# Routing's scatters paced to two under way, and no reads of keys within the projection

## The chip, the core and the metric

One NeuronCore of a Trainium2 chip. The metric is the time of one execution on the device in microseconds (us); times of a kernel are medians of several runs. TensorE does the matmuls, VectorE and ScalarE the elementwise work, GpSimd the rest and the indirect DMAs, SyncE (SP) issues most other DMAs.

## The reference

Two transformer layers over 4096 tokens of width 256, float32. What matters here is the first: adaptive layer norm, attention with 16 heads of 16 and a linear position bias, a residual, then a mixture of 64 experts (8 chosen per token, at most 256 tokens each) beside a shared expert.

```python
h = _layernorm(x) * (1 + ca) + sa
score = q @ k.T / sqrt(D) + bias          # 16 heads, 4096 x 4096
x = x + ga * (softmax(score) @ v)
h = _layernorm(x) * (1 + cb) + sb
topk_idx, topk_w = route(h)               # sigmoid, groups, 8 of 64 experts
xe = zeros(E, CAP, H).at[sorted_e, pos].set(tok_sorted)   # each token's row to 8 places
x = x + gb * (experts(xe) weighted + shared(h))
```

The second layer (rotary attention, gated linear attention) follows in other stages that the change doesn't touch.

## The kernel before

The program is a row of stages with a barrier of all engines between them: modulation, `project_heads`, `bias_attention`, `shared_expert`, `experts`, and those of the second layer. Each stage is a block with one hand-written queue of instructions per engine; waits on semaphores set the order.

**The projection** (`project_heads`) runs over 8 chunks of 512 tokens. TensorE computes queries and keys of a chunk in four parts (0 and 1 queries, 2 and 3 keys), ScalarE copies part b to `parts[b]` once its stores of the chunk before have landed (`parts_stored[b]`), VectorE writes the low half, and SP stores both halves to `q_laid` or `k_laid` in DRAM: eight DMAs of 256 KB a chunk, in the order of parts 2, 0, 1, 3 (`store`). Behind them SP waits for part 2's stores and reads the chunk's keys of the first head group back into `keys[0]` (`fetch`): four DMAs, 54 rows by two heads by 512 keys for each half. In the first chunk the first group's queries are read as well. ScalarE stores the values.

**The attention** (`bias_attention`) runs over 8 chunks of 512 queries (c) by 4 groups of 4 heads (g), 32 steps. Step s needs the row maxima of its scores: TensorE computes score tiles into two buffers (`ps_max`, L1023) and VectorE reduces each (L971), 64 tiles a step, 16 tiles ahead of the step before. Then VectorE turns the maxima, SP writes them to `m_rows` in DRAM and reads them back into the query rows (`set_rows`, L735 and L741), and only then TensorE can score (L1039), ScalarE take exps (L836) and TensorE multiply with the values (L1054). The maxima of the next step and the exps of this one are interleaved instruction by instruction on TensorE. SP loads keys for step s+2 and values for s+1 in quarters as they come free. Each DMA queue works in order. At the start SP loads the queries of group 1, the first values, the keys of group 1, the other values, then calls `set_rows(0, 0)`.

**Routing** of chunk c-1 runs beside chunk c's attention, from c = 1 to 7, mostly on GpSimd (`route`). Its last part is `send_rows` (L610): 4 x 8 indirect DMAs, each of which sends 128 rows (one per token, 320 floats) to their places in `x_rows`. They are issued one after another; then GpSimd waits for all. Chunk 7's routing is done in `shared_expert` with the same `send_rows`.

Of the kernel before, what the change touches and what calls it, by code (L numbers as in the profile page):

```python
# [7 lines left out]
P = 128  # L8
T = 4096
# [3 lines left out]
CH = 512  # L13
NC = T // CH
# [20 lines left out]
TOPK = 8  # L35
# [117 lines left out]
H0 = 16  # L153
# [61 lines left out]
def load_key_rows(sp, keys, k_laid, g, n, done):  # L215

    for h in range(2):
        src = k_laid[g * HG + h:(g + 1) * HG:2, :, n].rearrange("a r n -> r a n")
        at = h * HALF
        sp.dma_start(keys[at:at + LAID, :, n].bitcast(F32), src).then_inc(done, 16)  # L220
        sp.dma_start(keys[at + LAID:at + KROWS, :, n].bitcast(F32), src[AUX:AUX + HD0]).then_inc(done, 16)


def load_query_rows(sp, quer, q_laid, g, n, done):

    for h in range(2):
        src = q_laid[g * HG + h:(g + 1) * HG:2, :, n].rearrange("a r n -> r a n")
        at = h * HALF
        sp.dma_start(quer[at:at + AUX + HD0, :, :].bitcast(F32), src[0:AUX + HD0]).then_inc(done, 16)
        sp.dma_start(quer[at + AUX + HD0:at + KROWS, :, :].bitcast(F32), src[AUX:LAID]).then_inc(done, 16)  # L230


def project_heads(nc, xres, mod, ident, x_in, w_in, q_laid, k_laid, v_aug, k_aux, q_aux, keys, quer):

    with ExitStack() as ctx:
# [12 lines left out]
        w_loaded, aux_set, k_fetched, q_fetched = sem("w_loaded"), sem("aux_set"), sem("k_fetched"), sem("q_fetched")  # L248
# [9 lines left out]
        assert HG <= H0 // 2  # L258
        with nc.Block() as block:
            @block.sync  # L260
            def _(sp):
# [10 lines left out]
                def store(c):  # L272
                    for b in (2, 0, 1, 3):
# [23 lines left out]
                sp.wait_ge(q_fetched, 64)  # L297
                sp.wait_ge(k_fetched, 64 * NC)
# [382 lines left out]
def bias_attention(nc, q_laid, k_laid, m_rows, v_aug, x_rows, y_rows, hT_rows, xres, mod, ident, r, slots, w_router, e_bias,  # L681
                   first_keys, first_quer):


    with ExitStack() as ctx:
# [3 lines left out]
        keys = [first_keys, sb("keys1", [P, NPR, T], F32R)]  # L689
        quer = [first_quer] + [sb(f"quer{g}", [P, NPR, CH], F32R) for g in range(1, NG)]  # L690
# [20 lines left out]
         pos_set, slots_set, scattered) = (  # L711
            sem(n) for n in ("dve_step pool_step x_added stats_set pay_set h_stored r_exped scored opened mask_set "
                             "weighted wsum_set pos_set slots_set scattered").split())
# [4 lines left out]
        with nc.Block() as block:  # L718
            @block.sync
            def _(sp):  # L720
                def load_keys(g, b):
                    load_key_rows(sp, keys[g % 2], k_laid, g, slice(b * QUART * P, (b + 1) * QUART * P),
                                  k_loaded[g % 2][b])
# [2038 lines left out]
```

## Time and profile before

| | |
|---|---|
| median of 3 runs | 5701.97 us (5696.46 to 5717.44) |
| the profiled execution's own time, its span | 5714.75 us, 5713.2 us |
| TensorE busy | 4888.2 us (86%) |
| VectorE busy | 4150.3 us (73%) |
| ScalarE busy | 3063.1 us (54%) |
| GpSimd busy | 1115.6 us (20%) |
| mean DMA rate | 74 GB/s |

The projection begins at some 33 us and ends with the barrier before 247.7 us; the attention ends at about 3372 us. A busy share is a mean over all stages; the stages have different limits, so the rows further down are read by stretch. L-numbers are lines of the kernel. "Idle before" is what an engine waited just ahead of an instruction, with what ended the wait as the profile infers it; "remote" is an end that it can't tie to an instruction.

### The profile page before, as it was taken

The page shows a single profiled execution, that of the slowest core. Times are in us where ns is not written, and L with a number is a line of the kernel's source. Part 1 is how long each engine was busy: PE and PEld are TensorE (multiplying, and loading weights), DVE is VectorE, ACT ScalarE, POOL GpSimd, SP SyncE. Part 2 cuts the span into 40 slices and gives each one's busy share as a digit, 9 for nine tenths or more (in the row PEclk, how much of TensorE's full clock was granted, in tenths as well). Part 3 has the DMA queues.
Part 4 walks back from the last instruction along what each step waited for, and adds up shares of the span by engine and source line. Part 5 has one row for each costly group of instructions (what it writes and reads, how often), then busy time and mean ns, then how long its engine had stood idle before and what let it go on. Part 6 is the DMA issues. An engine that isn't in the chain of part 4 may idle for free. (4 is left out here: it accounts for less than half of the span.)

```text
span 5713.2 us, 110761 instructions
## 1 busy us (share of the span) xinstructions
PE 4888.2 (86%) x39176; PEld 2470.0 (43%) x39176; DVE 4150.3 (73%) x5059; ACT 3063.1 (54%) x5260; POOL 1115.6 (20%) x1152
## 2 busy tenths in 40 slices
PE   5489997997988979979989787845889987999998
PEld 3233332332333323323323234633556664666666
DVE  4398996996987979969979622336766554778877
ACT  1147876886777768858767661211222223555554
POOL 0000012102110121021111201034422001444443
PEclk8678998998998989989989898977999997999999
DMA  5424322222222212212222113752211012010100
GB/s 178 128 94 129 127 71 83 77 78 63 74 69 67 70 58 76 74 56 75 73 56 73 38 33 94 237 171 76 70 53 45 1 50 83 28 28 28 28 28 20
DMA packets 238050, 422.57 MB, mean 74 GB/s; under 512 B 36889, under 2 KB 141354, under 8 KB 237440
## 3 DMA queue, kind: packets, MB, share of 16 engines
q1 hardware_dynamic: 190688, 341.85, 19.8%
q0 software_dynamic: 30048, 66.76, 3.9%
q10 hardware_dynamic: 16896, 8.39, 0.6%
q8 instruction: 262, 4.29, 0.3%
q14 instruction: 156, 1.28, 0.1%
HBM read 324.51 MB, written 129.17 MB: 79 GB/s over the span
## 5 line engine op out<-in xcount | busy, mean ns | idle before, releaser
L971 DVE TENSOR_REDUCE attn_mpart<-attn_ps_max 128x2 f32<-128x1024 f32 x2048 | 2477.2, 1224 | 434.7 <-remote 213.8
L836 ACT ACTIVATE attn_probs<-attn_ps_exp 128x512 f32<-128x512 f32 x4096 | 2231.6, 595 | 770.7 <-PE attn_ps_exp L1039 342.0
L1039 PE MATMUL attn_ps_exp<-attn_quer,attn_keys 54*128 54x512 f32 x4096 | 1571.9, 461 | 204.3 <-issue 126.4
L1023 PE MATMUL attn_ps_max<-attn_keys,attn_quer 54*128 54x512 f32 x4096 | 1535.9, 475 | 127.6 <-DVE attn_mpart L971 71.3
L1054 PE MATMUL attn_ps_out<-attn_probs,attn_vals 128*32 128x256 f32 x16384 | 1356.1, 404 | 35.0 <-ACT attn_probs L836 16.3
L1039 PEld LDWEIGHTS attn_ps_exp<-attn_quer,attn_keys 54*128 54x128 f32 x4096 | 642.6, 191 | 1095.3 <-ACT attn_probs L836 872.3
L1023 PEld LDWEIGHTS attn_ps_max<-attn_keys,attn_quer 54*128 54x128 f32 x4096 | 619.2, 195 | 202.7 <-DVE attn_mpart L971 138.4
L1054 PEld LDWEIGHTS attn_ps_out<-attn_probs,attn_vals 128*32 128x32 f32 x16384 | 327.8, 109 | 799.2 <-issue 488.3
L1586 POOL DMA_INDIRECT ra_rows<-y_rows,slots x256 | 254.6, 994 | 360.9 <-DVE ra_total L1753 289.5
L1657 PE MATMUL ra_psO<-ra_vals,ra_probT 128*128 128x256 f32 x1152 | 280.7, 390 | 27.3 <-DVE ra_probT L1831 24.4
L1717 ACT ACTIVATE ra_row<-ra_psS 128x512 f32<-128x512 f32 x112 | 66.8, 597 | 388.9 <-PE ra_psS L1638 379.5
L610 POOL DMA_INDIRECT x_rows<-route_pay,route_now x256 | 251.9, 984 | 82.9 <-issue 75.5
L1638 PE MATMUL ra_psS<-ra_kT,ra_qT 128*128 128x512 f32 x576 | 258.9, 604 | 8.2 <-DVE ra_kT L1803 6.6
L2238 POOL TENSOR_TENSOR gla_ke<-gla_kg,emask 128x512 f32<-128x512 f32 x128 | 152.2, 1217 | 521.2 <-DVE gla_kg L2464 521.2
L1657 PEld LDWEIGHTS ra_psO<-ra_vals,ra_probT 128*128 128x128 f32 x1152 | 217.7, 196 | 75.1 <-DVE ra_probT L1831 30.1
L2529 PE MATMUL gla_psP<-gla_wqkv,gla_hc 128*128 128x512 f32 x384 | 194.2, 644 | 2.5 <-ACT gla_egn L2318 2.0
L800 POOL TENSOR_TENSOR route_tok<-route_tok,mod 128x1024 f32<-128x1024 f32 x7 | 16.7, 2381 | 900.0 <-DVE route_tok L480 900.0
L2224 POOL TENSOR_TENSOR gla_qeT<-gla_ftT,gla_emr 128x512 f32<-128x512 f32 x128 | 173.0, 1384 | 14.0 <-ACT gla_ftT L2270 14.0
L1831 DVE COPY ra_probT<-ra_psT 128x512 f32<-128x512 f32 x144 | 96.8, 689 | 108.4 <-PE ra_psT L1648 87.1
L1638 PEld LDWEIGHTS ra_psS<-ra_kT,ra_qT 128*128 128x128 f32 x576 | 109.3, 195 | 135.2 <-issue 124.2
L2323 ACT ACTIVATE gla_sq<-gla_psO 128x512 f32<-128x512 f32 x32 | 19.1, 597 | 266.4 <-PE gla_psO L2637 266.4
L1725 ACT ACTIVATE ra_row<-ra_row,ra_top 128x512 f32<-128x512 f32 (+7 forms) x32 | 70.9, 2216 | 160.7 <-DVE ra_top L1823 128.7
(367 smaller groups left out, 5413.9 us busy)
## 6 DMA issues: line engine op xcount, KB each, us to landing
attn_keys<-k_laid SPq DMA_DIRECT2D x248, 304.0 KB
attn_vals<-v_aug SPq DMA_DIRECT2D x128, 512.0 KB, 15.4
attn_keys<-k_laid SPq DMA_DIRECT2D x248, 128.0 KB
x_rows<-attn_zeros POOLq DMA_DIRECT2D x16, 1280.0 KB, 11.0
exp_x<-x_rows SPq DMA_DIRECT2D x64, 320.0 KB
exp_w1w<-in_w SPq DMA_DIRECT2D x64, 256.0 KB
y_rows<-exp_y SPq DMA_DIRECT2D x64, 256.0 KB
k_laid<-proj_parts SPq DMA_DIRECT2D x32, 256.0 KB
```

What stands on the lines that cost most here:

```text
L610: pool.indirect_dma_start(out=x_rows, out_offset=bass.IndirectOffsetOnAxis(ap=r.now[:, n, k:k + 1].bitcast(U32), axis=0), in_=r.pay[:, n, ...
L836: act.activation(probs[k % 2][:, j, :], ps_exp[bank_of(g, n)][:, :], ACT.Exp).then_inc(exp_done, 1)
L971: dve.tensor_reduce(mpart[i][:, kb, TC * pair + tile::TC * NPR], ps_max[buffer][:, :, :], AX, ALU.max).then_inc(unit_read, 1)
L1023: mm = pe.matmul(ps_max[buffer][:, h, :], quer[at % NG][half(h), pair, tile * P:(tile + 1) * P], keys[at % 2][half(h), pair, kb * CH:(kb + ...
L1039: pe.matmul(ps_exp[bank_of(g, n)][:, :], keys[g % 2][half(h), pair, k * P:(k + 1) * P], quer[g][half(h), pair, :], start=True, stop=True). ...
L1054: mm = pe.matmul(ps_out[j * VW:(j + 1) * VW, n], vals[:, k, j * VW:(j + 1) * VW], probs[k % 2][:, j, n], start=(k == 0 and q == 0), stop=( ...
L1586: pool.indirect_dma_start(out=rows[n % 2][:, k, :], out_offset=None, in_=y_rows, in_offset=bass.IndirectOffsetOnAxis(ap=slots[:, n, k:k + ...
L1638: mm = pe.matmul(psS[g % 2][:, :], qT[s // TC % 2][:, k, s % TC * P:(s % TC + 1) * P], kT[:, k, b * BLK:(b + 1) * BLK], start=(k == 0), st ...
L1657: mm = pe.matmul(psO[s % 2][:, :], probT[(before(s) + b) % 2][:, j * P:(j + 1) * P], vals[:, n, :], start=(n == 0), stop=(n == TC * blocks ...
L2224: last = pool.tensor_tensor(qeT[:, b, :, :], ftT[:, 3, b, :].unsqueeze(1).to_broadcast([P, NE, P]), emr[i][:, :, :], ALU.mult)
L2238: last = pool.tensor_tensor(ke[i][:, e, :], kg2[:, :], emask[:, bass.ds(m, 1), e].to_broadcast([P, KDV]), ALU.mult)
L2529: mm = pe.matmul(ps, hc[i][:, k, :], wqkv[:, x, k, :], start=(k == 0), stop=(k == KD - 1))
```

## The change

In the attention, `send_rows` gets a function `pace`: ahead of scatter i, from the third on, GpSimd waits until scatter i-2 has landed. For this the scatters count on two semaphores in turn. The shared expert's `send_rows` uses two semaphores too, without pacing. In the projection SP no longer reads keys and queries; it stores the parts in the order 0, 1, 2, 3. The attention's start loads the first group's queries and all its keys ahead of what it loaded before; `keys[0]` and `quer[0]` are allocated there. TensorE waits for them as for all others.

```diff
             def _(sp):
...
-                def store(c):
-                    for b in (2, 0, 1, 3):
+                with sp.Fori(0, NC) as c:
+                    for b in range(NB):
                         laid = q_laid if b < 2 else k_laid
                         hold(sp, qk_parts, NB * (c + 1) + b + 1, sp_passed)
                         for i in range(NPART):
...
-                def fetch(c):
-
-                    hold(sp, parts_stored[2], 16 * NPART * (c + 1), sp_passed)
-                    load_key_rows(sp, keys, k_laid, 0, bass.ds(c * CH, CH), k_fetched)
-
-                store(0)
-                sp.wait_ge(aux_set, 32)
-                for b in range(2):
-                    sp.wait_ge(parts_stored[b], 16 * NPART)
-                load_query_rows(sp, quer, q_laid, 0, slice(0, CH), q_fetched)
-                fetch(0)
-                with sp.Fori(1, NC) as c:
-                    store(c)
-                    fetch(c)
...
-def send_rows(pool, r, x_rows, scattered):
+def send_rows(pool, r, x_rows, scattered, pace=None):
 
     for n in range(TC):
         for k in range(TOPK):
+            if pace is not None:
+                pace(n * TOPK + k)
             pool.indirect_dma_start(out=x_rows, out_offset=bass.IndirectOffsetOnAxis(
                 ap=r.now[:, n, k:k + 1].bitcast(U32), axis=0), in_=r.pay[:, n, :], in_offset=None,
-                bounds_check=SLOTS - 1, oob_is_err=False).then_inc(scattered, 16)
+                bounds_check=SLOTS - 1, oob_is_err=False).then_inc(scattered[(n * TOPK + k) % 2], 16)
...
+                load_queries(0, 0)
+                for b in range(4):
+                    load_keys(0, b)
                 load_queries(0, 1)
                 load_vals(0, 0)
                 for b in range(4):
...
-                    send_rows(pool, r, x_rows, scattered)
-                    hold(pool, scattered, SENT * c, pool_passed)
+                    def two_under_way(i):
+                        if i >= 2:
+                            hold(pool, scattered[i % 2], SENT // 2 * (c - 1) + 16 * (i // 2), pool_passed)
+                    send_rows(pool, r, x_rows, scattered, two_under_way)
+                    for i in range(2):
+                        hold(pool, scattered[i], SENT // 2 * c, pool_passed)
```

## Rows read from the trace of the kernel before

**Rows 1.** The page: costliest group (busy us, mean ns | idle before)
```profile
L971 DVE TENSOR_REDUCE attn_mpart<-attn_ps_max 128x2 f32<-128x1024 f32 x2048 | 2477.2, 1224 | 434.7 <-remote 213.8
```
**Rows 2.** Windows: stretch, length; busy us by engine; clock, DMA share, GB/s
```profile
861.00:921.00 60.00, 59.33 (x569) 21.93 (x566) 59.02 (x59) 52.08 (x97) 6.14 (x13) 1.00 0.26 78
...
921.00:981.00 60.00, 29.28 (x171) 9.85 (x171) 17.61 (x19) 15.08 (x28) 31.56 (x32) 0.57 0.25 89
...
921.00:925.00 4.00, 4.00 (x37) 1.40 (x37) 3.19 (x3) 1.83 (x4) 3.12 (x3) 1.00 0.34 124
...
925.00:931.00 6.00, 3.06 (x24) 1.02 (x22) 1.88 (x2) 2.28 (x4) 4.71 (x5) 0.73 0.45 170
...
1690.00:1750.00 60.00, 29.10 (x196) 10.28 (x195) 21.04 (x22) 17.82 (x32) 31.52 (x32) 0.66 0.13 39
...
3245.00:3255.00 10.00, 2.94 (x12) 1.06 (x12) 1.23 (x1) 0.84 (x2) 7.76 (x8) 0.50 0.03 4
```
**Rows 3.** Timeline of GpSimd: start us, us; [idle before <- what ended it]
```profile
921.04 1.13 POOL L610 DMA_INDIRECT x_rows<-route_pay,route_now  x1 [1.00 <-POOL slots L820]
...
961.07 0.98 POOL L610 DMA_INDIRECT x_rows<-route_pay,route_now  x1 [0.30 <-issue]
...
1103.90 2.37 POOL L800 TENSOR_TENSOR route_tok<-route_tok,mod 128x1024 f32<-128x1024 f32 x1 [141.85 <-DVE route_tok L480]
...
3225.49 1.10 POOL L610 DMA_INDIRECT x_rows<-route_pay,route_now  x1 [0.93 <-POOL slots L820]
```
**Rows 4.** Timeline of VectorE after the first and the last burst
```profile
966.36 1.23 DVE L971 TENSOR_REDUCE attn_mpart<-attn_ps_max 128x2 f32<-128x1024 f32 x1 [5.92 <-remote]
...
3269.91 2.36 DVE L971 TENSOR_REDUCE attn_mpart<-attn_ps_max 128x2 f32<-128x1024 f32 x2 [21.18 <-remote]
```
**Rows 5.** Timeline of the rope stage, a burst of eight gathers
```profile
4285.14 1.01 POOL L1586 DMA_INDIRECT ra_rows<-y_rows,slots  x1 [26.47 <-DVE ra_total L1753]
...
4296.42 0.69 DVE L1831 COPY ra_probT<-ra_psT 128x512 f32<-128x512 f32 x1 [5.52 <-PE ra_psT L1648]
```
**Rows 6.** DMA: software queue in 961 to 963.3, all in 963.3 to 976
```profile
q0 software_dynamic: 96, 0.00, 3.0%
...
DMA packets 1, 0.02 MB, mean 1 GB/s; under 512 B 0, under 2 KB 0, under 8 KB 0
```
**Rows 7.** Timeline of the projection: SP's issues and one ScalarE copy
```profile
102.31 1.48 SPq L279 DMA_DIRECT2D k_laid<-proj_parts  x2
...
124.68 0.64 SPq L279 DMA_DIRECT2D k_laid<-proj_parts  x1
...
122.51 1.08 ACT L322 ACTIVATE proj_parts<-proj_psQ 128x512 fp32r<-128x512 f32 x2 [5.40 <-DMA q_laid<-proj_parts]
...
213.59 1.66 SPq L279 DMA_DIRECT2D k_laid<-proj_parts  x2
...
247.72 0.32 SPq L229 DMA_DIRECT2D attn_quer<-q_laid  x1
```
**Rows 8.** Timeline of the attention's start, and a later store of m_rows
```profile
257.71 1.22 PE L1023 MATMUL attn_ps_max<-attn_keys,attn_quer 54*128 54x512 f32 x4 [48.89 <-DMA route_e_bias_wide<-in_e_bias]
...
333.23 0.58 SPq L735 DMA_DIRECT2D m_rows<-attn_mturned  x1
...
335.29 0.62 SPq L741 DMA_DIRECT2D attn_quer<-m_rows  x2
...
349.18 1.28 ACT L836 ACT_TABLE_LOAD   x1 [131.79 <-PE attn_ps_exp L1039]
...
857.01 0.55 SPq L735 DMA_DIRECT2D m_rows<-attn_mturned  x1
...
869.76 0.60 SPq L741 DMA_DIRECT2D attn_quer<-m_rows  x2
```
**Rows 9.** Windows of a chunk of the projection and of the attention's start
```profile
102.30:124.70 22.40, 13.29 (x40) 7.39 (x40) 8.54 (x20) 4.44 (x9) 0.00 (x0) 0.92 0.57 163
...
316.00:333.00 17.00, 12.01 (x32) 4.42 (x30) 16.90 (x19) 0.00 (x0) 0.00 (x0) 0.50 0.00 0
```

More of the change, by code:

```diff
@@ L212, in chunk_pairs, with project_heads @@
     return go
[L215 to L233, printed above, removed]
+def project_heads(nc, xres, mod, ident, x_in, w_in, q_laid, k_laid, v_aug, k_aux, q_aux):
     with ExitStack() as ctx:
@@ L678, with bias_attention @@
 SENT = 16 * TC * TOPK
-def bias_attention(nc, q_laid, k_laid, m_rows, v_aug, x_rows, y_rows, hT_rows, xres, mod, ident, r, slots, w_router, e_bias,
-                   first_keys, first_quer):
+def bias_attention(nc, q_laid, k_laid, m_rows, v_aug, x_rows, y_rows, hT_rows, xres, mod, ident, r, slots, w_router, e_bias):
     with ExitStack() as ctx:
@@ L688, in bias_attention @@
         sem = ctx.enter_context(fresh_semaphores(nc, "attn_"))
-        keys = [first_keys, sb("keys1", [P, NPR, T], F32R)]
-        quer = [first_quer] + [sb(f"quer{g}", [P, NPR, CH], F32R) for g in range(1, NG)]
+        keys = [sb(f"keys{i}", [P, NPR, T], F32R) for i in range(2)]
+        quer = [sb(f"quer{g}", [P, NPR, CH], F32R) for g in range(NG)]
         vals = sb("vals", [P, NT, HG * VW])
@@ L721, in load_keys @@
                 def load_keys(g, b):
-                    load_key_rows(sp, keys[g % 2], k_laid, g, slice(b * QUART * P, (b + 1) * QUART * P),
-                                  k_loaded[g % 2][b])
-                def load_queries(c, g):
-                    load_query_rows(sp, quer[g], q_laid, g, bass.ds(c * CH, CH), q_loaded[g])
+                    i, n = g % 2, slice(b * QUART * P, (b + 1) * QUART * P)
+                    for h in range(2):
+                        src = k_laid[g * HG + h:(g + 1) * HG:2, :, n].rearrange("a r n -> r a n")
+                        at = h * HALF
+                        sp.dma_start(keys[i][at:at + LAID, :, n].bitcast(F32), src).then_inc(k_loaded[i][b], 16)
+                        sp.dma_start(keys[i][at + LAID:at + KROWS, :, n].bitcast(F32),
+                                     src[AUX:AUX + HD0]).then_inc(k_loaded[i][b], 16)
+                def load_queries(c, g):
+                    n = bass.ds(c * CH, CH)
+                    for h in range(2):
+                        src = q_laid[g * HG + h:(g + 1) * HG:2, :, n].rearrange("a r n -> r a n")
+                        at = h * HALF
+                        sp.dma_start(quer[g][at:at + AUX + HD0, :, :].bitcast(F32),
+                                     src[0:AUX + HD0]).then_inc(q_loaded[g], 16)
+                        sp.dma_start(quer[g][at + AUX + HD0:at + KROWS, :, :].bitcast(F32),
+                                     src[AUX:LAID]).then_inc(q_loaded[g], 16)
                 def load_vals(g, b):
@@ L1014, in unit_half @@
                     tile, pair = divmod(row, NPR)
-                    first = isinstance(c, int) and c == 0 and at == 0
-                    if u == 0 and not first:
-                        pe.wait_ge(q_loaded[at % NG], LQ * (c + at // NG + (1 if at % NG else 0)))
-                    if row == 0 and kb % 2 == 0 and not first:
-                        pe.wait_ge(k_loaded[at % 2][kb // 2], LK * (2 * (c + at // NG) + at % NG // 2 + at % 2))
+                    if u == 0:
+                        pe.wait_ge(q_loaded[at % NG], LQ * (c + at // NG + 1))
+                    if row == 0 and kb % 2 == 0:
+                        pe.wait_ge(k_loaded[at % 2][kb // 2], LK * (2 * (c + at // NG) + at % NG // 2 + 1))
                     place = unit_place(c, g, d, u)
@@ L1196, in _ @@
                 send_rows(pool, r, x_rows, scattered)
-                pool.wait_ge(scattered, SENT)
+                for i in range(2):
+                    pool.wait_ge(scattered[i], SENT // 2)
             @block.scalar
```

22 lines of the change are left out of this document (10 added, 12 removed).

## The prediction, made before the changed kernel was run

> **What bounds the kernel now.** I read the page first: the costliest group is VectorE's maxima over the score tiles [rows 1], 2048 at 1.22 us, 2477 us of a span of 5713. The windows then say how close to that the attention runs. In a calm minute (861 to 921 us) VectorE is busy 59.0 of 60 us, so a tile per 1.23 us is the pace, and what keeps a tile from VectorE takes 1.23 us from the kernel. The minute after it (921 to 981) has VectorE busy for 17.6 us only: 3.2 of the first 4, 1.9 of the next 6, and the granted clock averages 0.57 [rows 2]. That minute loses 60 - 17.6/0.984 = 42 us of the stream. The timeline tells what else happens in it: GpSimd sends routing's 32 scatters, the first at 921.04, then one every 0.98 + 0.30 = 1.28 us, the last at 961.07 [rows 3]. There are seven such bursts in the attention (224 of the program's 256 scatters; the last 32 stand in the shared expert); the third loses 60 - 21.0/0.984 = 39 us [rows 2], the others lie between. About 7 x 41 = 287 us stand in them, 5% of the kernel.
>
> **What the stall is.** It isn't transfer: in the last attention burst DMA is busy 3% of a stretch in which VectorE works 1.23 of 10 us [rows 2]. It isn't unfinished work either: the long waits end as "remote", and at a moment that goes by the scatters. After the first burst that is 966.36, after the last (first scatter 3225.49) it is 3269.91 [rows 3, 4]. Counted from the first scatter these are 45.3 and 44.4 us, 32 x 1.40. The rope stage's gathers come eight at a time: the first at 4285.14, and a VectorE copy that waited 5.52 us starts at 4296.42, 11.3 us on, which is 8 x 1.41 [rows 5]. I read it so: one indirect DMA occupies for about 1.4 us something that the engines' releases need too; they are issued every 1.28 us, so a backlog forms from the second on, and little gets past it until it is worked off. Three scatters still let 3.2/4 = 80% of the stream by, the next five 31% [rows 2], which fits a backlog and not a fixed toll. The mechanism is inferred; its end points are rows.
>
> **The change, part 1: pacing.** Removed: nothing. Added: before scatter i (i from 2) a wait of GpSimd until scatter i-2 has landed. Behind it on GpSimd's queue stand only the later scatters and the next chunk's routing. That starts at 1103.90, the last scatter at 961.07 [rows 3]: 142 us of room, so the burst may take up to 183 us, 5.7 us a scatter, and delay nobody.
> How far apart will they be? The software queue's packets of the scatter issued at 961.07 end before 963.3; after it only one instruction packet is seen until 976 [rows 6]. So landing takes at most 2.2 us from the start. From a release to the next scatter's start GpSimd needs 1.00 us (the idle time in front of 921.04 [rows 3]). Two under way then means two per 3.2 us, 1.6 us apart, above 1.41: the backlog drains. Key traffic now goes on beside them, so landing will take longer; I allow 3.4 us, 2.2 us apart (estimate). In the middle, 1.8, a burst takes 58 us instead of 41. What share of the stream lives in it? The bounds are the 31% and the 80% above [rows 2]; I take 55%, the middle, since two of 1.4 us fill most of each 3.6 us. Lost per burst 58 x 0.45 = 26 us against 41: seven times 15 is **-105 us**. The ends: 80% over 50 us loses 10 (-217 in all), 31% over 58 loses 40 (-7). The 32 scatters of the shared expert aren't paced; their second semaphore costs nothing, since nobody waits before the end.
> The Trainium skill ("DMA: Bandwidth & Descriptors", Anatomy of one DMA) gives a DMA issued from GpSimd 2.0 us plus its bytes over 436 GB/s; for 128 rows of 1280 B that is an estimate of 2.4 us. The trace's bound of 2.2 us is near it, and by 2.4 the distance would be 1.7 us, the sum the same.
>
> **Part 2, the projection without reads.** A chunk now takes 22.4 us (SP's first store at 102.31, then 124.68) [rows 7]; in each, SP issues four key reads behind the eight stores. What these cost in the queue shows in the attention: a store of 16 KB (m_rows) is back after 2.1 us on an empty queue (333.23 to 335.29) and after 12.8 behind one quarter of keys (857.01 to 869.76) [rows 8]. A chunk is half a quarter, 6.4 us on the DMA engines that carry it; every store behind it in order is late by that, and ScalarE's copies wait for the stores (5.40 us at 122.51 [rows 7]). So 22.4 - 6.4 = 16 us without them. The lower bound by transfer: DMA is busy 57% of a chunk [rows 9], 12.8 us, of which the reads are an eighth (0.43 of 3.5 MB): 11. I take 17, between 15.5 and 20. The first store of a chunk now needs part 0 and not part 2, about 5 us earlier, once. From the last chunk's first store (213.59) to the attention's first DMA (247.72) it is 34.1 us [rows 7]; less the last two chunks' reads, 21. Sum over six intervals: 6 x 5.4 + 5 + 13 = 50 us (27 to 60).
>
> **Part 2, the attention's start.** The first score matmul now runs 10.0 us after the barrier (257.71, against SP's 247.72; released by GpSimd's small loads), m_rows goes out 85.5 us after it, and ScalarE turns to exp (its table load) at 349.18, +101.5, when sixteen tiles of the next group are done [rows 8]. SP's loads keep DMA busy until 316 (nothing from 316 to 333 [rows 9]): 68 us for four quarters of keys, queries and values. After the change the first group's queries and first quarter must come first, 12.8 us plus queries and latency: first matmul at about +21. Worse: four more quarters, 51 to 56 us, stand ahead of m_rows. TensorE and VectorE have only the sixteen tiles as cover, gone at +111 (+21 and the 91 us from 257.71 to 349.18). SP can hand m_rows over by +107, but in order it lands after the loads, at 68 + 51 to 56 + 4 for queries, about +126. Exp starts at about +131 instead of +101.5: **+30 us** (+11 if m_rows slips past, +35 at most). SP's keys for the third group are asked for after exp has begun, so the delay is paid once.
> Net of part 2: 30 - 50 = **-20 us**, between -45 and +10.
>
> **Sum.** -105 - 20 = -125. The profiled execution took 5714.75 us, span 5713.2; the median of the three timed runs is 5702, 12.8 lower. Against the median: **5577 us**.
>
> **Rivals.**
> *Pacing stops the stall altogether* (17%). For it: once nothing is queued, releases might never be late. Against: even three scatters cost a fifth. 7 x -36 and -20 give 5432; with something lost, up to 5490.
> *Pacing changes nothing* (15%). Landing in at most 2.2 us [rows 6] is less than 2 x 1.28: two under way is nearly true already, the wait may be free and the cadence stay. Then only part 2 counts: 5682, 5660 to 5712. Against it stands the 1.00 us of restart [rows 3], if GpSimd can't look ahead past a wait. The Trainium skill ("SBUF — State Buffer", SBUF: two separate sides) says that a compute operation and a DMA can't slow each other at SBUF; by it no number of scatters under way would matter. The stretch at 3% DMA [rows 2] agrees that it isn't SBUF, but there the engines do stand still.
> *The paced bursts are longer and stall as before* (18%; the other side). Place: the seven bursts. If each scatter holds the releases until the next is issued, the backlog is not the cause, and a burst of 32 x 1.6 + 4 = 55 us stands as the 45 do now: 7 x 9.5 = +67, less 20: 5749. It decides where the stream in a 58 us burst stays below 29% of its pace (42 us lost). For it: with the stream dead no keys load, so landing stays quick and the scatters close.
> *Part 2 costs* (5%): if ScalarE's or SP's own order keeps a chunk at 21 us, the projection gives 8 + 5 + 6 = 19 and the start takes 30: +11, and 5608 with the pacing, 5713 without.
>
> **How the numbers follow.** The forecast (partial relief) has 45%, its own range 5465 to 5690. About 0.5% (28 us) is what a measurement of this kernel can tell from none. Faster by more: nearly all of the 45, 17, and a little of the rest, 62%. Within: most of "changes nothing" and the edges, 18%. Slower: the 18 and some of part 2's, 20%. For 8 in 10 the range leaves out the lower half of the full relief and the top of the slower case: 5440 to 5745.
>
> **What would show it.** In the changed profile: scatters 1.6 to 2.2 us apart in the seven bursts and 1.28 in the shared expert; VectorE near 55% in a burst and few remote waits over 5 us; SP's first stores of chunks 16 to 20 us apart; the first group's m_rows over 15 us on its way, TensorE idle before the first exp. A cadence of 1.28 us with the same stall, or the same stall at 1.6, would prove part 1 wrong; chunks still at 22 us, part 2.

## The result and the profile after

The changed kernel took 5460.41 us (median of 4 runs, 5440.40 to 5491.74) against 5705.52 us (median of 4, 5696.46 to 5717.44): a ratio of 0.9559, 95% interval 0.9522 to 0.9596. That is 245 us less, where the prediction had 125 us less as the likeliest and 5440 to 5745 as its range. The profiled execution took 5440.40 us, span 5438.8; its span is 274.4 us below that of the profiled execution before.

The page's costliest groups after the change (line, engine and operation | busy us, mean ns | idle us before it and what ended it):

```profile
L956 DVE TENSOR_REDUCE attn_mpart<-attn_ps_max 128x2 f32<-128x1024 f32 x2048 | 2468.3, 1224 | 205.9 <-PE attn_ps_max L1007 188.3
...
L577 POOL DMA_INDIRECT x_rows<-route_pay,route_now x256 | 252.4, 986 | 455.5 <-DMA x_rows<-route_pay,route_now 375.9
```

VectorE's maxima are the same work (1224 ns each, as in [rows 1]), but the idle time in front of them falls from 434.7 to 205.9 us: 229 us less in that one row, and the 213.8 us of "remote" are no longer named. GpSimd now waits 376 us for the landings of its own scatters. Windows of the changed kernel, for a calm minute, the first two bursts, the last one in the attention and the stretch behind it (length; busy us of TensorE's matmuls, its weight loads, VectorE, ScalarE and GpSimd; granted clock, DMA share, GB/s):

```profile
841.00:901.00 60.00, 59.50 (x567) 21.93 (x567) 58.98 (x58) 52.02 (x97) 6.14 (x13) 1.00 0.28 78
901.00:1009.00 108.00, 105.29 (x991) 39.31 (x995) 101.59 (x93) 88.97 (x166) 31.61 (x32) 1.00 0.37 114
1250.00:1356.00 106.00, 104.27 (x984) 38.90 (x983) 100.67 (x92) 88.70 (x164) 31.01 (x32) 1.00 0.31 87
2992.00:3047.00 55.00, 53.64 (x455) 20.13 (x452) 15.73 (x17) 45.33 (x87) 31.44 (x32) 1.00 0.10 25
...
3047.00:3070.00 23.00, 23.00 (x210) 8.74 (x209) 0.00 (x0) 21.58 (x42) 0.00 (x0) 1.00 0.01 1
```

Read the first burst against the stretch from 921 to 981 in [rows 2]: VectorE is busy 101.59 of 108 us where it was busy 17.6 of 60, and TensorE keeps its clock of 1.00 where it had 0.57. At the calm pace of 58.98 in 60 the 108 us would hold 106.2, so a burst now loses 4.6 us of the stream, the second one 3.5, instead of 41. But the bursts are 107 us long, not 58. GpSimd's timeline shows how they go:

```profile
901.35 1.13 POOL L577 DMA_INDIRECT x_rows<-route_pay,route_now  x1 [0.99 <-POOL slots L801]
902.79 1.01 POOL L577 DMA_INDIRECT x_rows<-route_pay,route_now  x1 [0.30 <-issue]
908.16 0.98 POOL L577 DMA_INDIRECT x_rows<-route_pay,route_now  x1 [4.36 <-DMA x_rows<-route_pay,route_now]
909.45 0.98 POOL L577 DMA_INDIRECT x_rows<-route_pay,route_now  x1 [0.30 <-issue]
...
1008.00 0.98 POOL L577 DMA_INDIRECT x_rows<-route_pay,route_now  x1 [5.56 <-DMA x_rows<-route_pay,route_now]
1049.33 2.39 POOL L781 TENSOR_TENSOR route_tok<-route_tok,mod 128x1024 f32<-128x1024 f32 x1 [40.34 <-DVE route_tok L445]
```

Scatters go in pairs 1.3 to 1.4 us apart, then mostly a wait of some 4 to 6 us for a landing: (1008.00 - 901.35)/31 = 3.44 us on average in the first burst. The six bursts with key loads beside them have 3.0 to 3.4 us; the seventh has no keys to load (DMA share 0.10 in the window above) and has 1.75.

The bursts also differ in how many rows they move. Where a token's expert has its 256 tokens already, `chosen_slots` gives a place past the end of `x_rows`, and the scatter leaves that row out. The DMA view's row of the software queue (packets, MB, share) has, in the kernel before, from 921 to 963.5 and from 3225.4 to 3268, and in the changed kernel from 1250.4 to 1361:

```profile
q0 software_dynamic: 1536, 4.39, 28.4%
...
q0 software_dynamic: 1536, 0.23, 3.5%
...
q0 software_dynamic: 1536, 1.40, 4.1%
```

So the first burst moved 4.39 MB and the last 0.23, and both stalled alike (45.3 and 44.4 us). It is the number of scatters in a given time that stalls the engines, not the bytes. Nor do the bytes set the distance of the paced bursts: the second to the sixth move only 1.40 to 0.35 MB and still have 3.0 to 3.4 us. What they have and the seventh has not are the key loads (7.9 MB of other DMAs in the second burst, 1.1 in the seventh).

The DMA packets in the traces also tell when a scatter lands. In the seventh burst of the kernel before, the packets that raise a scatter's semaphore end 1.8 to 2.0 us after its issue, for all 32. At 1.29 us apart that is 1.4 scatters under way on average, never three. The changed kernel has the same 1.8 us there (28 of the 32 within 2.0, four between 2.1 and 3.1), a distance of 1.75, and no stall.

The room until the next chunk's routing (1049.33) has shrunk from the 142 us of [rows 3] to 40.

The projection and the start of the attention, SP's issues and ScalarE's first table load:

```profile
206.03 0.35 SPq L701 DMA_DIRECT2D attn_quer<-q_laid  x1
...
315.20 1.11 SPq L713 DMA_DIRECT2D m_rows<-attn_mturned  x1
335.14 0.62 SPq L719 DMA_DIRECT2D attn_quer<-m_rows  x2
...
338.10 1.28 ACT L821 ACT_TABLE_LOAD   x1 [153.66 <-PE attn_ps_exp L1023]
```

Beside [rows 7, 8]: the attention's first DMA goes out at 206.03 instead of 247.72, the first exponentials at 338.10 instead of 349.18. The maxima's way through m_rows takes 19.9 us instead of 2.1, and TensorE waits 20.3 us for it.

Where the 274 us of the span are, by landmarks of the two timelines: the first scatter is 19.7 us earlier (921.04 to 901.35). From there to the seventh burst's first scatter (3225.49 before, 2991.85 after) it takes 2090.5 us instead of 2304.4, 213.9 less, or 35.7 in each of six intervals. From that scatter to the shared expert's table load (3386.4 before, 3118.5 after) it takes 126.6 instead of 160.9 us, 34.3 less. That is 248 us in seven bursts. Behind it 6.5 us are left.

### The profile page after: what moved, and what is told of

It reads as the page before. It is cut to its first block and busy times, and to the rows that moved or that the text cites. A ratio compares the mean times of both kernels' runs of the same rounds, so it can differ in the third digit from the quotient of the medians.

```text
span 5438.8 us, 111021 instructions
## 1 busy us (share of the span) xinstructions
PE 4828.8 (89%) x39176; PEld 2459.1 (45%) x39176; DVE 4139.9 (76%) x5059; ACT 3059.3 (56%) x5260; POOL 1117.3 (21%) x1152
## 3 DMA queue, kind: packets, MB, share of 16 engines
q14 instruction: 156, 1.28, 0.1%
## 5 line engine op out<-in xcount | busy, mean ns | idle before, releaser
L956 DVE TENSOR_REDUCE attn_mpart<-attn_ps_max 128x2 f32<-128x1024 f32 x2048 | 2468.3, 1224 | 205.9 <-PE attn_ps_max L1007 188.3
L1023 PE MATMUL attn_ps_exp<-attn_quer,attn_keys 54*128 54x512 f32 x4096 | 1552.8, 455 | 62.5 <-DMA attn_quer<-m_rows 38.3
L1007 PE MATMUL attn_ps_max<-attn_keys,attn_quer 54*128 54x512 f32 x4096 | 1512.0, 469 | 108.1 <-DVE attn_mpart L956 61.4
L1038 PE MATMUL attn_ps_out<-attn_probs,attn_vals 128*32 128x256 f32 x16384 | 1335.2, 398 | 7.5 <-ACT route_o L826 6.0
L1443 DVE TENSOR_TENSOR exp_hidden<-exp_psU,exp_gate 128x256 f32<-128x256 f32 x64 | 27.2, 425 | 162.4 <-PE exp_psY L1496 157.6
```

The source lines that it names most:

```text
L956: dve.tensor_reduce(mpart[i][:, kb, TC * pair + tile::TC * NPR], ps_max[buffer][:, :, :], AX, ALU.max).then_inc(unit_read, 1)
L1007: mm = pe.matmul(ps_max[buffer][:, h, :], quer[at % NG][half(h), pair, tile * P:(tile + 1) * P], keys[at % 2][half(h), pair, kb * CH:(kb + ...
L1023: pe.matmul(ps_exp[bank_of(g, n)][:, :], keys[g % 2][half(h), pair, k * P:(k + 1) * P], quer[g][half(h), pair, :], start=True, stop=True). ...
L1038: mm = pe.matmul(ps_out[j * VW:(j + 1) * VW, n], vals[:, k, j * VW:(j + 1) * VW], probs[k % 2][:, j, n], start=(k == 0 and q == 0), stop=( ...
```

## The experiments

Twelve further runs were made, all of them with the whole computation; two are the kernels before and after once more, and one is a repeat. They came to four chips, and the chip turned out to matter; the kernel before was timed beside each of them on its own chip. The table's last column is the time from the first scatter of the first burst to that of the seventh, six chunks, by GpSimd's timeline.

| kernel | chip | before there | this one | ratio (95%) | six chunks |
|---|---|---|---|---|---|
| the first runs of before / changed | not on record | 5705.52 | 5460.41 | 0.9559 (0.9522 to 0.9596) | 2304.4 / 2090.5 |
| pace_only | 12 | 5729.83 | 5523.29 | 0.9639 (0.9603 to 0.9674) | 2120.0 |
| reads_only | 12 | 5729.83 | 5722.27 | 0.9984 (0.9956 to 1.0012) | 2315.5 |
| memset_between | 12 | 5729.83 | 5444.35 | 0.9500 (0.9461 to 0.9539) | 2095.1 |
| one_under_way | 12 | 5729.83 | 5604.21 | 0.9780 (0.9744 to 0.9815) | 2234.7 |
| before_again | 7 | 5721.97 | 5728.72 (one run) | | 2311.0 |
| after_again | 7 | 5721.97 | 5535.49 | 0.9650 (0.9597 to 0.9703) | 2132.8 |
| memset_every_fourth | 11 | 5383.02 | 5386.24 | 1.0015 (0.9998 to 1.0032) | 2085.8 |
| four_under_way | 11 | 5383.02 | 5381.46 | 0.9994 (0.9976 to 1.0013) | 2091.6 |
| shared_spaced | 11 | 5383.02 | 5376.30 | 0.9988 (0.9963 to 1.0014) | 2072.5 |
| rows_by_act | 11 | 5383.02 | 5354.87 | 0.9940 (0.9917 to 0.9964) | 2090.9 |
| best | 15 | 5382.61 | 5358.95 | 0.9960 (0.9942 to 0.9978) | 2087.2 |
| memset_fourth_again | 15 | 5382.61 | 5379.69 | 0.9989 (0.9971 to 1.0006) | 2096.7 |

**The two parts apart.** The kernel before with the pacing alone:

```
-                    send_rows(pool, r, x_rows, scattered)
-                    hold(pool, scattered, SENT * c, pool_passed)
+                    def two_under_way(i):
+                        if i >= 2:
+                            hold(pool, scattered[i % 2], SENT // 2 * (c - 1) + 16 * (i // 2), pool_passed)
+                    send_rows(pool, r, x_rows, scattered, two_under_way)
+                    for i in range(2):
+                        hold(pool, scattered[i], SENT // 2 * c, pool_passed)
```

> The kernel before with the pacing alone: two semaphores in turn, a wait for the landing of scatter i-2 ahead of scatter i, the reads within the projection kept. Theory A (the pacing gives all but some 11 to 20 us of the gain; each of the seven bursts loses 3 to 4 us of the stream in place of 41): 5705 - 250 = about 5455, and the first exponential still 101 us after the barrier. Rival B (the gain needs the later start or the freed loads of the projection as well, so that the parts are not additive): above 5500.

And the changed kernel without it:

```
-                    def two_under_way(i):
-                        if i >= 2:
-                            hold(pool, scattered[i % 2], SENT // 2 * (c - 1) + 16 * (i // 2), pool_passed)
-                    send_rows(pool, r, x_rows, scattered, two_under_way)
+                    send_rows(pool, r, x_rows, scattered)
```

> The changed kernel without its waits between scatters: the two semaphores stay, the 32 scatters of a burst go out back to back, and the projection has no reads. Theory A (the two semaphores by themselves do nothing, the projection's part is worth 41.7 us at the barrier less 30.6 us at the start, plus up to 9 us before the first burst): 5685 to 5695, bursts 40 us long with 41 us lost in each. Rival B (two semaphores in turn relieve the backlog even unpaced): under 5600, and exponentials that go on through the bursts.

Without the waits the stall is back in full, two semaphores or one. A window of reads_only over its first burst (892.0 to 932.1):

```profile
892.00:933.00 41.00, 12.19 (x75) 4.12 (x75) 6.87 (x6) 6.01 (x11) 31.50 (x32) 0.62 0.33 121
```

6.87 of 41 us for VectorE. So the pacing is what counts, and the projection's part is worth at most a few us: 7.6 by the medians, within what can't be told from nothing. Its first exponentials came at 331.41 (changed kernel 338.10, before 349.18), so 11 to 18 us are there in the traces, and the times show less.

pace_only missed its number: 5523, where 5455 was expected and 5500 was given as the mark of parts that need each other. The trace says otherwise. Its scatters are 2.7 to 3.5 us apart in the first six bursts, and the stream goes on beside them as in the changed kernel. From the seventh burst to the table load (3029.7 to 3196.6), however, it takes 166.9 us, where the changed kernel took 126.6. Windows of pace_only there:

```profile
3064.00:3068.00 4.00, 3.32 (x29) 1.23 (x21) 0.00 (x0) 2.39 (x5) 2.41 (x3) 1.00 0.02 0
3068.00:3072.00 4.00, 3.95 (x22) 1.31 (x21) 0.00 (x0) 3.14 (x7) 1.93 (x3) 0.62 0.04 4
...
3085.00:3110.00 25.00, 25.00 (x150) 7.03 (x142) 0.00 (x0) 15.93 (x30) 0.00 (x0) 0.50 0.01 1
```

From 3085 on, behind the last scatter, TensorE is busy all the time at a granted clock of 0.50 (1.2 GHz) and does 150 matmuls in 25 us. The changed kernel had 210 in 23 us at 1.00 in the same work (the last of its windows above). Those 40 us are TensorE's clock, which fell at about 3070, behind a stretch with 3.32 us busy of 4, and was low for most of the time until the table load. Such a stretch isn't enough by itself: the changed kernel's first profile has one with 3.45 of 4 (3030 to 3034) and kept 1.00. That this isn't a matter of the projection's reads shows in the changed kernel itself, below. With the 40 us taken off, pace_only is 247 us below the kernel before by the medians. Its six chunks are also 30 us longer than in the changed kernel's first profile. That is the clock again: over the six chunks TensorE does the same matmuls, and is busy 2051.9 us for them instead of 2023.2.

**Distance or number under way?** A memset of GpSimd (128x320) between two scatters, and no wait for a landing:

```
+                    def later(i):
+                        if i >= 1:
+                            for j in range(1):
+                                pool.memset(idle[:, :], 0.0).then_inc(idle_set, 1)
+                                hold(pool, idle_set, 31 * 1 * (c - 1) + 1 * (i - 1) + j + 1, pool_passed)
...
-                    send_rows(pool, r, x_rows, scattered, two_under_way)
+                    send_rows(pool, r, x_rows, scattered, later)
```

> The changed kernel with one GpSimd memset of a tile of its own (128x320, 0.36 us by the memset of the same shape before) and its semaphore between two scatters, in place of the wait for a landing: scatters come 1.7 to 1.8 us apart whether or not they have landed, a burst takes about 55 us in place of 105. Theory R (rate: what brings the releases is kept busy 1.4 us by each scatter, and above that distance there is no backlog, however many are under way): stall gone, 5450 to 5475, no slower than with two under way by more than 15 us. Theory N (number under way: the stall comes when many are in flight, and under the stream's load a landing takes 4 to 6 us, so three or more are): the stall is back in part, 5550 or more. Theory S (my forecast's share: each scatter takes 1.4 us from the stream): 20% of 55 us is left to it, 44 us lost in each burst, about 5700.

GpSimd's timeline and the windows of the first two bursts:

```profile
903.79 1.01 POOL L577 DMA_INDIRECT x_rows<-route_pay,route_now  x1 [0.89 <-POOL attn_idle L806]
904.78 0.41 POOL L806 MEMSET attn_idle<- 128x320 f32 x1
906.07 0.98 POOL L577 DMA_INDIRECT x_rows<-route_pay,route_now  x1 [0.88 <-POOL attn_idle L806]
```
```profile
901.00:973.00 72.00, 68.08 (x619) 24.99 (x623) 64.17 (x58) 56.56 (x104) 43.39 (x63) 0.93 0.42 131
1252.00:1324.00 72.00, 69.71 (x626) 25.53 (x627) 65.03 (x58) 57.39 (x106) 43.35 (x63) 0.93 0.31 90
```

The scatters come 2.26 us apart (more than the 1.8 expected: the memset begins only when the scatter's 1.0 us are over, and 0.9 us pass behind it), whether they have landed or not. The stall is gone all the same: 72 us at the calm pace would be 70.8, VectorE has 64.2 and 65.0, so some 6 us are lost. At a ratio of 0.9500 the kernel is at least as fast as the changed one (0.9559, on another chip). Theory N is out: by the packets in the first burst a landing takes some 4 us here, so about two are under way, and that is more than the 1.4 of the kernel before's last burst, which stalls. Theory S, my own forecast's idea of a share, is out too. By it the stream would have had 38% of the burst, (2.25 - 1.40)/2.25. It had over 90%.

**One under way.** One semaphore, and the wait for scatter i-1:

```
-                        if i >= 2:
-                            hold(pool, scattered[i % 2], SENT // 2 * (c - 1) + 16 * (i // 2), pool_passed)
...
+                        if i >= 1:
+                            hold(pool, scattered[i % 1], SENT // 1 * (c - 1) + 16 * (i // 1), pool_passed)
```

> The changed kernel with one semaphore and the wait for the scatter just before, so that one is under way. Pairs 1.28 us apart are gone; each scatter waits for a landing of 3 to 6 us, and the last ends at 32 x 5 to 6 = 160 to 190 us, past the 145 us that lie between the first scatter and the next chunk's routing. Theory A (what is left of the loss, 3 to 4 us in each burst, is from the pairs): as the changed kernel or 10 to 20 us faster if the routing behind is not on the path; later routing may delay GpSimd's own next chunk by 20 to 40 us, which the extra places in TensorE's queue would turn into waits: up to 5600. Theory N (landing takes as long as there is a pair to serve): scatters 2.5 to 3 us apart, 80 to 95 us in all, 5450 to 5460.

5.77 us apart, a burst of 179 us, and 160 us slower than memset_between on the same chip. VectorE's timeline of this kernel shows the end of the room that the changed kernel has 40 us of:

```profile
1097.01 1.41 DVE L452 BATCH_NORM_STATS2 route_stats<-route_tok 128x6 f32<-128x256 f32 x4 [21.57 <-POOL route_tok L782]
```

GpSimd issues its last scatter at 1088.92 and begins the next chunk's routing at 1091.91 instead of 1049.33; the row statistics, which stand at a fixed place in VectorE's queue, wait 21.57 us for it (20.7 to 26.0 in the next four chunks), and the maxima behind them too. GpSimd's own chain, 179 us of scatters and 195 us of the rest, then sets the chunk: 374 us (1284.1 less 910.2). The expectation's "up to 5600" was the right branch (5604).

**A chip without the stall.** Four kernels ran together next, on chip 11. memset_every_fourth has this in place of the wait for a landing:

```
+                        if i and i % 4 == 0:
+                            pool.memset(idle[:, :], 0.0).then_inc(idle_set, 1)
+                            hold(pool, idle_set, 7 * (c - 1) + i // 4, pool_passed)
```

four_under_way, with four semaphores in turn:

```
+                        if i >= 4:
+                            hold(pool, scattered[i % 4], SENT // 4 * (c - 1) + 16 * (i // 4), pool_passed)
```

shared_spaced is memset_between with this in the shared expert as well:

```
+                def later(i):
+                    if i >= 1:
+                        pool.memset(idle[:, :], 0.0).then_inc(idle_set, 1)
+                        pool.wait_ge(idle_set, i)
-                send_rows(pool, r, x_rows, scattered)
+                send_rows(pool, r, x_rows, scattered, later)
```

And rows_by_act, the changed kernel with this in ScalarE's queue ahead of its first exponential, and without SyncE's set_rows(0, 0):

```
+                act.wait_ge(rows_turned, 1)
+                act.dma_start(m_rows.rearrange("(ct b i) -> b ct i", b=4, i=P // 4),
+                              mturned[:, :]).then_inc(rows_stored, 16)
+                act.wait_ge(rows_stored, 16)
+                for h in range(2):
+                    rows = m_rows.rearrange("(h r q) -> h r q", h=2, q=CH)[h]
+                    at = slice(h * HALF + BIAS, h * HALF + AUX)
+                    act.dma_start(quer[0][at, :, :].bitcast(F32),
+                                  rows.unsqueeze(1).to_broadcast([AUX - BIAS, NPR, CH])).then_inc(rows_loaded, 16)
```

> As the kernel with a memset between scatters, but with the memset ahead of every fourth scatter only: distances of 1.28, 1.28, 1.28 and 2.25 us, on average 1.52 us, a burst of 47 us. The distance of 2.25 us ended the stall and 1.28 us has it in full; this one lies just above the 1.40 us that a scatter of the kernel before took to serve. Theory R (a threshold at 1.40 us on average): the stall shrinks to the pieces of three or four scatters, under 10 us in each burst, 5450 to 5500. Theory G (what the stream gets is the time that the scatters leave, distance less 1.40 us, and the stream needs about 0.2 us of each of its own 1.2 us or so for its releases): 8% is left, a third to a half of what the stream wants, 25 to 30 us lost in each burst, 5600 to 5650.

> The changed kernel with four semaphores in turn and the wait for scatter i-4, so that up to four are under way. Theory R (only the mean distance counts; the wait for the landing of the oldest sets it): the scatters land behind each other, 1.4 us each when nothing else is served, and the distance depends on how much of the stream gets between. If the queue of four is never empty, the stream is starved as before: distance 1.4 to 1.6 us, 5650 or more. Theory B (a landing waits for its turn behind the stream's own releases, as the 4 to 7 us waits with two under way show, so four under way share with the stream): distance 1.8 to 2.5 us, bursts of 60 to 80 us, 5450 to 5500.

> The kernel with a memset between scatters, which also has the memset between the 32 scatters of the shared expert's burst (those were back to back in every kernel so far). In the changed kernel VectorE stands for 28.6 us there, until 5.6 us after the last scatter, and TensorE for 20 us. Theory A (the same stall, on the path): this burst becomes 72 us and the stream goes on beside it; 20 to 30 us faster than with the memset in the attention alone, 5415 to 5425. Rival (the experts behind wait for the last scatter, 32 us later than now): no gain, or up to 10 us slower.

> The changed kernel with the first block's maxima (m_rows) stored and read back by ScalarE's queue at the start of the attention, instead of SyncE's, where they wait behind 40 key loads. The transpose is done at 301.4 and the store goes out at 315.2 and is back at 335.1; the loads of the second group's keys are issued until 311.9. Theory A (the delay is SyncE's queue and the loads that stand ahead of it): the store goes out at 301.5, first exponential at 306 to 312 in place of 339; PE's 20.3 us wait is gone, 20 to 28 us faster than the changed kernel, 5435 to 5440. Rival (the DMA engines have the key rows ahead of it whatever queue it comes from): store back at 325 or later, under 10 us gained.

On this chip the unchanged kernel before took 5383 us, 25 times between 5366 and 5403, and the first three took as long: ratios of 1.0015, 0.9994 and 0.9988. With no stall to end they could not decide between their theories. (The 0.2 us that theory G gives the stream's releases is an assumption; no run shows it.) What they do show is that the stall is absent here. The shared expert's 32 scatters are back to back, 1.28 us apart, in memset_between (chip 12) as in memset_every_fourth (chip 11). One window of each over that burst:

```profile
3143.00:3183.00 40.00, 22.68 (x64) 12.29 (x62) 6.33 (x10) 1.79 (x3) 30.56 (x32) 0.80 0.08 19
```
```profile
3130.00:3174.00 44.00, 37.28 (x104) 20.43 (x105) 18.51 (x37) 3.58 (x6) 30.53 (x32) 0.92 0.11 30
```

On chip 12 TensorE is busy 57% of the time and ScalarE gets 3 operations done; on chip 11 it is 85% and 6 (the 4 us ahead of the burst included). In the first profile of the changed kernel VectorE stands still there for 28.57 us, until 5.5 us after the last scatter:

```profile
3188.63 1.29 DVE L1213 TENSOR_TENSOR disp_actT<-disp_psU,disp_gate 128x512 f32<-128x512 f32 x2 [28.57 <-DMA attn_quer<-m_rows]
```

In memset_every_fourth no wait of VectorE over that burst is longer than 9.7 us. The same scatters at the same distance stop the engines on one chip and not on the other. The gathers of the rope stage differ too: from the first to the last of the 256 it takes 613 to 623 us in the eight profiles of the slower chips (the first runs' among them), 571 to 578 in the six of chips 11 and 15.

rows_by_act gained where it was meant to. ScalarE's timeline:

```profile
299.51 1.13 ACTq L847 DMA_DIRECT2D m_rows<-attn_mturned  x1
309.94 0.66 ACTq L853 DMA_DIRECT2D attn_quer<-m_rows  x2
318.30 1.28 ACT L822 ACT_TABLE_LOAD   x1 [132.93 <-PE attn_ps_exp L1033]
```

The store is back in 10.4 us instead of 19.9, TensorE's wait for it falls from 20.3 to 2.4 us, and the kernel is 27 us faster than four_under_way beside it (the time of the changed kernel wasn't measured on this chip). Both theories were partly right: the queue was most of it, but with SyncE's key loads still being issued (until 310) the store takes 8 us more than the 2.1 of [rows 8], so the exponentials start at 318 and not at 306 to 312.

**The two kernels again, and a better one.**

> The kernel before, unchanged, profiled again, because in the comparison with the memset ahead of every fourth scatter it took 5383 us (25 runs, 5366 to 5403) where its other runs took 5696 to 5783. Theory C (the stall in the bursts belongs to the chip on which the kernel runs, not to the kernel alone): on a chip where the time is near 5383 the seven bursts of back-to-back scatters leave the stream nearly untouched (VectorE over 85% busy through them, chunk period near 345 us), and on one where it is near 5710 each loses 41 us again (chunk period 384 us). Rival D (something else of the kernel, such as the projection or the experts, is faster there): the bursts lose 41 us in both, and the 320 us are elsewhere.

> The changed kernel, unchanged, beside the kernel before on the same chip. Theory C: if the kernel before takes near 5710 here, the ratio is again 0.956; if it takes near 5383, the pacing has nothing to win, and only the projection's part and the start are left, 11 to 20 us: ratio 0.995 to 1.00, 5360 to 5385. Rival D: 0.956 in either case.

These fell on chip 7, where the kernel before takes 5722. It stalls in its bursts (intervals of 382 to 389 us from one to the next) as at first. The changed kernel was 3.5% faster and not 4.4, with runs from 5486 to 5558. Its profiled execution shows the loss of pace_only in the changed kernel itself, from 3093 to 3195, clock 0.53:

```profile
3093.00:3195.00 102.00, 94.90 (x553) 28.29 (x554) 6.68 (x18) 57.36 (x106) 0.80 (x2) 0.53 0.07 23
```

The stall came back (theory C), and the spread that neither theory had is TensorE's clock: from the seventh burst to the shared expert's first scatter it takes 186.0 us here and 151.5 in the first profile, 35 us more. The 42 us in the six chunks are the clock as well. TensorE is busy 2062.0 us in them instead of 2023.2, 38.8 more for the same number of matmuls. One chunk of the first profile and the same one here:

```profile
1941.67:2288.43 346.76, 335.10 (x3116) 126.81 (x3117) 326.71 (x333) 280.89 (x518) 59.33 (x66) 0.99 0.27 76
...
1966.86:2328.41 361.55, 347.64 (x3116) 130.09 (x3117) 327.73 (x333) 280.98 (x518) 59.31 (x65) 0.94 0.25 73
```

Over the whole program TensorE is busy 4922.8 us in this execution and 4828.8 in the first one, 94 of the 117 us between their spans; so most of the difference between the two is its clock. Why it fell more often in the second isn't shown.

One thing can't be told apart from the chip: each chip was used at one time only, so that the stall may go with the chip or with something else that differed then.

best is memset_between with the shared expert's memsets and ScalarE's m_rows, edits shown above.

> Three changes at once: the memset between scatters in the attention, the same in the shared expert, and the first block's maxima by ScalarE's queue. On a chip where the kernel before takes near 5720 and loses 41 us in each burst: 5445 of the memset kernel, less 20 to 28 for the shared expert's burst, less 18 for the start, about 5400 (5385 to 5430; up to 5480 if TensorE's clock stays low at the end of the attention as in the profile of the changed kernel's second run), ratio 0.942 to 0.95. On a chip where it takes near 5383: only the start's 18 to 28 us and nothing from the bursts, 5345 to 5360, ratio 0.993 to 0.996.

> The memset ahead of every fourth scatter once more, mean distance 1.52 us, because its first run fell on a chip on which even back-to-back scatters do not stop the stream. On a chip where the kernel before takes near 5720: theory R (a threshold at the 1.40 us that one scatter occupies): under 10 us lost in each burst, 5450 to 5500. Theory G (the stream gets what the scatters leave of the time, 8% here): 25 to 30 us lost in each burst of 47, 5600 to 5650. On a chip where it takes near 5383: no difference again.

Both ran on a chip of the faster kind (chip 15, before 5382.61). best took 5358.95, 0.44% below before, which is the size of the start's share; the expectation for such a chip was 5345 to 5360. It is the fastest but for rows_by_act (5354.87 on chip 11), and the two can't be told apart. What it brings on a chip that stalls wasn't measured, nor was the distance of 1.52 us there.

## Why the prediction was right, and where it was not

**The stall and its cause** held, as far as experiments reach. Seven bursts lost about 41 us each, scatters at 1.28 us were what did it (reads_only stalls, pace_only and memset_between don't), and wider distances end it. Shown is the distance, and neither the bytes nor the number under way; where the stall occurs, the closest that ran free of it is the seventh burst's 1.75 us. That one scatter takes 1.40 us of something that the releases need stays inferred, and what that something is isn't known: at 1.28 us the DMA engines themselves kept up (a landing in 1.8 us throughout the last burst). A distance between 1.28 and 1.75 was never tried where the stall occurs.

**Part 1 was mis-sized: -105 us forecast, -248 measured.** The direction was right, and so was the means (distance between the scatters). Two terms of the sum were wrong.

The distance: 1.8 us forecast, 3.0 to 3.4 measured. The 2.2 us for a landing came from [rows 6], after a burst in which the stream had stood still, so that no keys were being loaded beside the scatter. (That scatter moved no row at all: its 96 packets make 0.00 MB. The prediction set it beside an estimate for 128 full rows. The bursts with few rows show that this didn't matter.) With the stream running, DMA share 0.31 to 0.37, the waits were mostly 4 to 6 us. In the seventh burst, share 0.10, the distance was 1.75: there the forecast of 1.8 was right. A latency was read in the very state that the change removes.

The share of the stream in a burst: 55% forecast, 96% measured (101.59 of 106.2). I took the 31% and 80% of [rows 2] as bounds, but both come from scatters issued back to back. At the wider distances no backlog shows at all, and there was no share to take: even at 2.25 us, where a proportional toll leaves 38%, the stream kept over 90%. The rival "pacing stops the stall altogether" (17%, 5432, up to 5490) is what happened; its "-36 per burst" is the measured 35.4 (248/7). My objection to it, that even three scatters cost a fifth, was drawn from scatters issued back to back. (Its terms, 7 x 36 and 20 from 5702, give 5430, not 5432.) The share is the term that carries the miss. With 96% in the forecast's burst of 58 us the loss is 2 us; with 55% in the real burst of 107 us it would have been 48, more than the 41 of the kernel before.

The range held partly by luck: 5460 lies outside the forecast's own branch (5465 to 5690) and inside the stated range only because that took in half of a rival with 17%.

**Room.** That a burst "may take up to 183 us" and delay nobody was worked out with 142 us of room, part of which the stall itself had made. In the changed kernel 148 us lie between the first scatter and the next chunk's routing (901.35 to 1049.33), and that is the bound, 4.6 us a scatter. The paced bursts take up to 107 us and leave 40; at 179 us (one_under_way), still below 183, VectorE waits 21 to 26 us in each chunk for GpSimd.

**Part 2: -20 forecast.** By the trace: the barrier 41.7 us earlier, against 50 forecast, with chunks of 17.5 us on average (SyncE's first stores at 56.25 and 178.57, seven intervals), as foreseen (17). Exp at +132.1 behind SP's first DMA (forecast +131, before +101.5), so +30.6 at the start, against +30. Net -11 at the first exponential, -20 at the first scatter. In the times reads_only shows 0.16% less, interval 0.44% less to 0.12% more, so "worth little" is shown and its sign isn't. That m_rows would stand behind the loads was the best forecast of all, and rows_by_act shows that it is some 20 of the 30 us (exponentials at 318.30 instead of 338.10).

**Changes nothing** (the second rival) had its ground right, as the landing in 1.8 us shows: in the last burst two under way was true already. But the wait for a landing still stretched the distance there from 1.29 to 1.75 us, by the restart that the prediction set against this rival, and the stall was gone. On the faster chips, where there was no stall to end, kernels with wider distances gained nothing. The rule of the Trainium skill that it weighed ("SBUF — State Buffer", SBUF: two separate sides) speaks of the way to SBUF. The trace agrees that this isn't where it happens, since a burst of 0.23 MB stalls like one of 4.39; but the number of scatters in a given time did matter, 4% of the kernel.

**Longer bursts that stall as before** had longer bursts right (107 us at most; it had 55) and the stall wrong. The prediction's estimate of 2.4 us for a scatter of 128 full rows, from the Trainium skill ("DMA: Bandwidth & Descriptors", Anatomy of one DMA), was met by no wait beside key loads: there 4 to 6 us stand between the pairs. Without key loads a landing takes 2.2 us in the first burst of the kernel before, from its eleventh scatter on, and 1.8 in the seventh with its few rows.

## What to carry to other kernels

If the engines stand still during a run of GpSimd's indirect DMAs while DMA is nearly idle, put distance between the DMAs, by a wait for a landing or just by other work of GpSimd. Both took the stall away (six chunks in 2090.5 and 2095.1 us instead of 2304.4), and the cheap filler kept the burst shorter (70 against 107 us) and so more of the room behind it. Don't pace harder than needed: with one under way GpSimd became the bound. And take a latency for such a sum from a stretch in which the traffic of the changed kernel runs, not from one that the stall has emptied.

## What the hardware showed that was not expected

The chip matters. The same kernel before took 5722 and 5730 us on two chips and 5383 on two others. The stall in the bursts and 40 us of the gathers' stage are what differ in the traces (the kernel before itself was profiled only on the slower kind, so for the faster kind this rests on its time and on the back-to-back burst of the kernels beside it). What gained 3.6 to 5.0% on one chip (pace_only, memset_between) gained nothing measurable on another (shared_spaced, four_under_way); the changed kernel itself wasn't timed there. What differs between the chips, and whether it is the chip or the time of the run, isn't known.

TensorE's granted clock can stay at 0.50 (1.2 GHz) for some 100 us while TensorE is busy nearly all the time (pace_only from 3072 to 3180, with 150 matmuls in 25.00 busy us of 25). The fall came behind stretches of 3.3 busy us in 4. It cost 35 to 40 us in pace_only and in one profile of the changed kernel, and wasn't there in the other profile of the same kernel; lower clocks within the chunks cost 30 to 40 us more. It makes two runs of one kernel differ by more than part 2 of the change is worth.
